# Two mixer stages in one program: a new order of transpositions, output product, weighted inputs and state in each supertile, and first loads issued beside the constants

## What is computed

```python
proj = norm(x) @ in_proj_w             # columns: z (1024) | x, B, C | dt
xBC  = silu(conv4(proj_xBC) + conv_b)  # causal, 4 taps, one filter per channel
dt   = softplus(dt + dt_bias); dA = exp(-exp(A_log) * dt)
state = state * dA_t + outer(dt_t * x_t, B_t)      # per head, along the sequence
y_t   = C_t @ state + D * x_t
out   = (rmsnorm(y) * silu(z)) @ out_proj_w        # A: rmsnorm(y * silu(z))
```

## Time and profile before

| what | value |
|---|---|
| median of 3 runs (lowest to highest) | 3190.09 us (3183.87 to 3195.75) |
| the profiled execution: its own time, its span | 3185.51 us, 3183.8 us |
| TensorE busy | 2839.6 us, 89% |
| VectorE, ScalarE, GpSimd busy | 65%, 39%, 31% |
| mean granted TensorE clock | 0.953 |
| mixer A: its first load, its last output product | 9.97 us, about 1210 us |
| mixer B: its first load, its last output product | 1461.90 us, about 2936 us |

### The profile page before, as it was taken

One profiled execution on the slowest core, in us unless ns is written; L12 is line 12 of the kernel. 1 busy time (PEld: TensorE's weight loads), 2 busy tenths in 40 slices (PEclk: granted clock), 3 DMA queues, 4 the chain that ended last, 5 costly groups with the idle time before them and its releaser, 6 DMA issues. The chain is left out here.

```text
span 3183.8 us, 54365 instructions
## 1 busy us (share of the span) xinstructions
PE 2839.6 (89%) x19824; PEld 1872.3 (59%) x19824; DVE 2071.5 (65%) x3697; ACT 1248.4 (39%) x2098; POOL 975.0 (31%) x618
## 2 busy tenths in 40 slices
PE   4999999999999996993899999999999999997896
PEld 4666666666666663453666666666666666664453
DVE  3565665665566562485777777877777777776267
ACT  2433434334443331331444444444444444443232
POOL 1232222332233230251233332333233333223135
PEclk9999999999999998996899999999999999998898
DMA  3000000000000005144000000000000000000533
GB/s 117 14 20 26 20 20 20 20 26 26 20 20 20 20 14 225 52 147 158 11 21 20 20 13 20 20 20 10 16 20 20 20 20 13 13 15 29 217 104 134
DMA packets 80673, 140.16 MB, mean 44 GB/s; under 512 B 18120, under 2 KB 18632, under 8 KB 79568
## 3 DMA queue, kind: packets, MB, share of 16 engines
q1 hardware_dynamic: 60048, 126.29, 11.2%
q10 hardware_dynamic: 20544, 12.79, 1.5%
HBM read 104.98 MB, written 33.55 MB: 44 GB/s over the span
## 5 line engine op out<-in xcount | busy, mean ns | idle before, releaser
L525 PE MATMUL work<-b_xnT,b_w_in 128*128 128x256 f32 x2304 | 564.6, 397 | 39.9 <-DVE b_state L1096 29.2
L525 PE MATMUL work<-a_xnT,a_w_in 128*128 128x256 f32 x2176 | 505.0, 388 | 10.0 <-DVE a_w_out L1227 5.8
L525 PEld LDWEIGHTS work<-b_xnT,b_w_in 128*128 128x128 f32 x2304 | 434.5, 195 | 127.8 <-DVE b_state L1096 36.0
L525 PEld LDWEIGHTS work<-a_xnT,a_w_in 128*128 128x128 f32 x2176 | 411.6, 193 | 83.1 <-issue 18.1
L1081 DVE TENSOR_TENSOR b_decay<-b_decay,b_gt 128x1024 f32<-128x1024 f32 x256 | 340.1, 1366 | 27.4 <-ACT b_decay L799 23.4
L799 ACT ACTIVATE b_decay<-seg 128x1024 f32<-128x1024 f32 x256 | 251.6, 1022 | 201.6 <-PE seg L649 200.9
L960 DVE SCALAR_TENSOR_TENSOR b_cv<-b_pre,b_conv_w,b_cv 128x256 f32<-128x256 f32 x480 | 249.6, 548 | 58.8 <-ACT b_cv L745 50.9
L1286 POOL TENSOR_TENSOR a_y<-a_y,a_skip 128x1024 f32<-128x1024 f32 x32 | 106.5, 3327 | 548.2 <-DVE a_y L1070 548.2
L1251 POOL TENSOR_TENSOR rhs<-b_l_side,of_head 128x1024 fp32r<-128x1024 f32 x32 | 83.2, 2600 | 609.3 <-DVE b_l_side L1050 609.3
L630 PE MATMUL work<-a_w_out,a_yz 128*128 128x512 f32 x512 | 248.8, 642 | 21.8 <-ACT a_xnT L729 18.1
L630 PE MATMUL work<-b_w_out,b_yz 128*128 128x512 f32 x512 | 230.8, 604 | 23.7 <-ACT b_xnT L729 15.6
(11 more groups left out here) (309 smaller groups left out, 4733.4 us busy)
## 6 DMA issues: line engine op xcount, KB each, us to landing
f_d_w<-in_L_ffn_d_w SPq DMA_DIRECT2D x4, 4096.0 KB, 24.0
f_x_in<-x_mid ACTq DMA_DIRECT2D x12, 1024.0 KB, 5.9
a_x_in<-in_L_attn_a_x SPq DMA_DIRECT2D x16, 512.0 KB, 3.7
a_x_res<-in_L_attn_a_x SPq DMA_DIRECT2D x32, 256.0 KB, 2.6
x_mid<-a_x_res SPq DMA_DIRECT2D x32, 256.0 KB, 2.0
f_x_res<-x_mid SPq DMA_DIRECT2D x8, 1024.0 KB, 5.5
f_bc_w<-x_mid SPq DMA_DIRECT2D x8, 1024.0 KB, 5.4
b_x_in<-x_mid SPq DMA_DIRECT2D x16, 512.0 KB, 3.6
```

The costliest lines, as they stand in the source:

```text
L525: mm = nc.tensor.matmul(dst, w_in[:, k, col:col + m], xnT[:, k, :], start=(k == 0), stop=(k == KD - 1))
```

## The change

1. TensorE's head becomes `xnT0, pout, xnT1, ident0, small1` (then `dt`). `pout` now has the bank of `prt`, `xnT1` that of `xnT0`, `small1` that of `pout`, and `dt` that of `xnT1`. `ident0` was after the first projections. ScalarE does `slot_exp(0,1)` between its two copies.
2. `state0` comes before the last `ydiag` steps of tile 0, and `state_add(0)` before `gate(0)`.
3. VectorE makes `xdt` of tile 0 right behind `masked_gt`, and that of tile 1 ahead of the first `slot_mult`.
4. `w_out` is multiplied by `norm_w` in the first supertile, at the place of `out_add`; TensorE waits for it before the first output product only.
5. A's `x_in` and `w_in` are issued on SyncE's queue inside the block of constants, and A's six vectors on ScalarE's queue there. The loads of `masks`, of F's 12 vectors and of B's six vectors go to SyncE's queue behind the second `x_in` and the first residual load of A. B issues no vector loads at its start. Both prologues transpose and copy `xn` before they wait for weights or vectors.

```diff
+def load_vectors(eng, dst, w, H, loaded):
+    for name in ("dt_bias", "A_log", "D"):
+        eng.dma_start(dst[name][:], w[name].rearrange("(a h) -> a h", a=1).to_broadcast([P, H])).then_inc(loaded, 16)
...
+def load_in(sp, x_in, w_in, xs_src, w, x_loaded, xbc_loaded):
+    sp.dma_start(x_in[:], xs_src[0]).then_inc(x_loaded, 16)
+    sp.dma_start(w_in[:, :, E:], w["in_proj"].rearrange("(t p) n -> p t n", p=P)[:, :, E:]).then_inc(xbc_loaded, 16)
...
     with nc.Block() as block:
+        @block.sync
+        def _(sp):
+            w = weights[mixers[0].tag]
+            load_in(sp, early["x_in"], early["w_in"], early["xs_src"], w, early["x_loaded"], early["xbc_loaded"])
+            load_z(sp, early["w_in"], w, early["z_loaded"])
...
+                load_vectors(act, c["vectors"][m.tag], weights[m.tag], m.H, c["vectors_loaded"][m.tag])
...
-                    + (["xnT0", "xnT1"] if nxt else []) + (["pout"] if prev else []) + ["small1"])
+                    + (["xnT0"] if nxt else []) + (["pout"] if prev else []) + (["xnT1"] if nxt else [])
+                    + ["ident0", "small1"])
...
-                if p == 0:
-                    steps += ["ident0"]
+                if p + 1 == NP:
+                    steps += state_steps(0)
                 steps += [f"ydiag0.{2 * p}", f"ydiag0.{2 * p + 1}"]
-            steps += (["z0a"] if nxt else []) + state_steps(0)
+            steps += ["z0a"] if nxt else []
...
                 load_x(1)
                 load_res(0, 0)
+                if later:
...
+                        load_ffn_vectors(sp, c["ffn"], c["ffn_w"], c["ffn_loaded"])
+                        load_vectors(sp, c["vectors"][later.tag], c["weights"][later.tag], later.H,
+                                     c["vectors_loaded"][later.tag])
...
+                        if isinstance(i, int) and i == 0:
+                            pe.wait_ge(w_out_ready, 1)
...
+                run(prologue(), pro_steps[:2])
                 pe.wait_ge(xbc_loaded, 16)
...
-                pe.wait_ge(w_out_ready, 1)
                 pe.wait_ge(c["masks_loaded"], 16 * 16)
...
                         xnT_copy(sec, 0)
+                    slot_exp(sec, 0, 1)
+                    if nxt:
                         xnT_copy(sec, 1)
-                    slot_exp(sec, 0, 1)
...
                     masked_gt(sec)
+                    make_xdt(sec, 0)
...
-                    make_xdt(sec, 0)
+                    make_xdt(sec, 1)
                     slot_mult(sec, 0, 0)
...
                     slot_mult(sec, 0, 1)
-                    make_xdt(sec, 1)
                     if prev:
                         out_add(sec, "pout", i - 1, 1)
+                    else:
+                        norm_into_w_out()
...
+                                state_add(sec, 0)
                                 gate(sec, 0)
```

More of the change, by code:

```diff
@@ L188, in build_constants, with mixer_phase @@
     return c
-def mixer_phase(nc, sig, before, cfg, c, first_mixer, psum, x_src, x_dst, w):
+def mixer_phase(nc, sig, before, cfg, c, early, later, psum, x_src, x_dst, w):
     H, HP, N, NS = cfg.H, cfg.HP, cfg.N, cfg.slots
@@ L213, in sb @@
             return ctx.enter_context(nc.sbuf_tensor(f"{cfg.tag}_{name}", shape, dt))
-        w_in = sb("w_in", [P, KD, cfg.proj])
+        w_in = early["w_in"] if early else sb("w_in", [P, KD, cfg.proj])
         w_out = sb("w_out", [P, KE, DM])
-        conv_w = sb("conv_w", [P, NB, TAPS])
-        conv_b = sb("conv_b", [P, NB])
-        norm_w = sb("norm_w", [P, KE])
-        dt_bias = sb("dt_bias", [P, H])
-        a_log = sb("a_log", [P, H])
+        conv_w, conv_b, norm_w, dt_bias, a_log, d_skip = (c["vectors"][cfg.tag][k] for k in (
+            "conv_w", "conv_b", "norm_w", "dt_bias", "A_log", "D"))
+        small_loaded = c["vectors_loaded"][cfg.tag]
         a_low, a_high = sb("a_low", [P, H]), sb("a_high", [P, H])
-        d_skip = sb("d_skip", [P, H])
-        x_in = sb("x_in", [P, 2, DM])
+        lhs, rhs = sb("lhs", [P, 2, P], F32R), [sb(f"rhs{k}", [P, 8, P], F32R) for k in range(2)]
+        x_in = early["x_in"] if early else sb("x_in", [P, 2, DM])
         x_res = sb("x_res", [P, 2, DM])
@@ L509, in _ @@
                 load_res(0, 0)
+                if later:
+                    for b in range(4):
+                        for q in range(4):
+                            sp.dma_start(c["masks"][32 * q:32 * q + 32, b], c["masked_bf"][32 * b:32 * b + 32]
+                                         ).then_inc(c["masks_loaded"], 16)
+                    with nc.allow_non_contiguous_dma(reason="small vectors"):
+                        load_ffn_vectors(sp, c["ffn"], c["ffn_w"], c["ffn_loaded"])
+                        load_vectors(sp, c["vectors"][later.tag], c["weights"][later.tag], later.H,
+                                     c["vectors_loaded"][later.tag])
                 before.clear(sp)
@@ L1128, in out_add, with norm_into_w_out @@
                                                    ).then_inc(out_done, 1)
+                def norm_into_w_out():
+                    dve.wait_ge(out_loaded, 16)
+                    for k in range(KE):
+                        ins = nc.vector.tensor_scalar(w_out[:, k, :], w_out[:, k, :], norm_w[:, k:k + 1], None, ALU.mult)
+                    ins.then_inc(w_out_ready, 1)
                 def supertile(sec, prev, nxt):
@@ L1224, in _ @@
                 exponent_sides(0)
-                dve.wait_ge(out_loaded, 16)
-                for k in range(KE):
-                    ins = nc.vector.tensor_scalar(w_out[:, k, :], w_out[:, k, :], norm_w[:, k:k + 1], None, ALU.mult)
-                ins.then_inc(w_out_ready, 1)
                 supertile(first(), False, True)
@@ L1894, in build, with first_mixer_buffers @@
         }
-        c = build_constants(nc, ctx, part("L0_ffn_"))
         mixer_signals, ffn_signals = Signals(nc, ctx, "m"), Signals(nc, ctx, "f")
         route = [x0] + x_mid[:len(STAGES) - 1] + [y]
+        weights = {"a": part("L0_attn_a_"), "b": part("L0_attn_b_")}
+        first = ExitStack()
+        def first_mixer_buffers():
+            return {"masked_bf": first.enter_context(nc.sbuf_tensor("masked_bf", [P, 4, P], BF16)),
+                    "x_in": first.enter_context(nc.sbuf_tensor("a_x_in", [P, 2, DM], F32)),
+                    "w_in": first.enter_context(nc.sbuf_tensor("a_w_in", [P, KD, mixer_a.proj], F32)),
+                    "xs_src": x0.rearrange("(s j p) d -> s p j d", p=P, j=2),
+                    "x_loaded": mixer_signals("x_loaded"), "xbc_loaded": mixer_signals("xbc_loaded"),
+                    "z_loaded": mixer_signals("z_loaded")}
+        c = build_constants(nc, ctx, part("L0_ffn_"), (mixer_a, mixer_b), weights, first_mixer_buffers)
         for k, stage in enumerate(STAGES):
@@ L1900, in build @@
             if stage == "A":
-                mixer_phase(nc, mixer_signals, ffn_signals, mixer_a, c, True, psum, src, dst, part("L0_attn_a_"))
+                with first:
+                    mixer_phase(nc, mixer_signals, ffn_signals, mixer_a, c, c["early"], mixer_b, psum, src, dst, weights["a"])
             elif stage == "B":
-                mixer_phase(nc, mixer_signals, ffn_signals, mixer_b, c, False, psum, src, dst, part("L0_attn_b_"))
+                mixer_phase(nc, mixer_signals, ffn_signals, mixer_b, c, None, None, psum, src, dst, weights["b"])
             else:
```

76 lines of the change are left out of this document (38 added, 38 removed).

## The result

The changed kernel takes 3009.26 us, the median of 4 runs (3007.08 to 3011.85). The kernel before took 3189.41 us beside it (4 runs, 3183.87 to 3195.75). The ratio is 0.9435, with a 95% interval from 0.9416 to 0.9454: 180 us less, where 152 had been forecast. The time lies a microsecond above the low end of the range. The profiled execution took 3011.85 us (span 3010.1), against 3185.51 before: 173.7 us less. The comparison by stages is made between these two.

A forecast was written before the change was run, and what follows sets the result against it. TensorE was taken to bound both loops. Waits 82, clock 30, prologue ends 12, start of B 15.5 and start of A 12 sum to 151.5 us off 3185.5: 3034, or 3038 as median; range 3008 to 3100.

The forecast's parts named there:

- start of B: B's first projection no longer waits for vectors landing at 1489.48, only for `w_in`: 15.5 us gained.
- waits in the loops: TensorE's waits for the `xnT` copy, `out_add` and `state_add` go in both loops: 82 us, ends 60 and 87.
- clock in the loops: Falls of TensorE's clock behind waits cost 39.9 us; a quarter stays: gain 30 us, ends 0 and 45.
- ends of the prologues: TensorE no longer waits for `w_out` there: 6 us in A, 8 in B, together 12 after the multiplications, ends 6 and 14.
- start of A: Loads issued inside the block of constants bring A's first projection to 25 to 29 us: gain 12, ends 8 and 18.
- Head, TensorE's side: At each supertile's head, `pout` hides the `xnT` copy, 33.7 us; the waits of `dt` for `out_add` go, 25.5 us.
- the cover of 0.3 us in A: In A's head VectorE finishes its last `slot_mult` 0.3 us before `pout` would end, so `out_add` is hidden.
- a late VectorE: Rival: VectorE is late for `out_add`, `small1` waits, 0.9 us in 28 supertiles, 25 us come back: 3063, chance 0.14.
- State of tile 0: `state0` and its add moved earlier give `z0b` its bank in time; B's waits for `state_add`, 27.3 us, go.
- a wait of `state0b` and a late `rs0` reader: New delays in B's loop behind ScalarE's copy and the convolutions: 0.3 us per supertile, 4 us in all.
- The second rival: The clock falls in each loop supertile's head, 1.7 us each; the 30 us gain becomes a loss of 8: 3076, chance 0.14.

## Why the prediction was right, and where its sizes were off

The sign, the mechanism and the range held, the range by a microsecond and with luck: the stages for which the forecast had no term lost 8.6 us, and without that loss the time would lie below its low end. The start of B left the bounds of its own term. The forecast's terms against the stages measured:

| term | forecast | measured |
|---|---|---|
| waits in the loops | 82 (60 to 87) | 86.6 |
| clock in the loops | 30 (0 to 45) | 39.9 |
| busy time at full clock | none | 11.2 |
| ends of the prologues, with the first supertiles | 12 (6 to 14) | 4.6 + 7.4 − 2.4 + 1.3 = 10.9 |
| start of B | 15.5 (13 to 18) | 19.1 |
| start of A | 12 (8 to 18) | 14.5 |
| the two F, last supertiles, end | none | −8.6 |
| sum | 151.5 | 173.6 |

**Head, TensorE's side.** Right: no wait for the copy, none for `out_add`, the cover of 0.3 us in A measured 0.35. In B the slot multiplication started later than reckoned, behind both halves of `xdt(1)` and the first slot, and the margin was 0.24 us instead of 1.0. It held in both. What the prediction made too little of is what stood on it: it priced a late VectorE at 25 us; the run with the old `xdt` order lost 118. The 0.9 us assumed for it there was 1.2 and 2.3, and the clock, which that rival left out, cost more than the wait.

**State of tile 0.** The 27.3 us went, and so did the falls behind them (13 us in the run with the step undone). The 4 us put down for a wait of `state0b` and a late `rs0` reader did not come: that is nearly the whole of 86.6 − 82.

**The clock.** This is the step that was mis-sized. A quarter of the falls was to stay: none stayed, 39.9 us against 30 (48, by the second profile of the kernel before). The reason given, the row in which `small1` and `dt` were followed by half clock, read the row for its products; it had half a microsecond of waiting in it, behind a longer wait at 590 us. The runs separate the two. The same head with one pause more falls in every supertile of A; with 32 transpositions more and no pause more, in none; with 0.4 us of pause among the small products and `ident0` gone from them, in 4 of 28. The second rival (a fall in each head, 3076 us), which the rule of the Trainium skill on transpose mode, cited above, would give, is refuted by the changed kernel and by the run with more transpositions.

**Busy time at full clock.** A term that was missing: TensorE's busy time of an undisturbed supertile fell by 0.48 and 0.32 us. The forecast took a wait's own length for its cost; 11.2 us on 86.6 come on top, and their cause stays open.

**Ends of the prologues.** At the transpositions the gain was 4.6 + 7.4 = 12.0 us, where 6 + 8 had been forecast. And the multiplications were said to cost 1.6 us in A and nothing in B where they went. They took 5.68 and 4.92 us, against 3.26 and 3.25 in the run that has them later: at the new place GpSimd works beside them, for 3.0 us in A (state and skip part) and for 1.9 in B (state), at the later one it doesn't. `small_sums(1)` behind them made TensorE wait 4.7 and 3.9 us. The run that moved them won back 4.8 us of TensorE's wait in A's first supertile and 5.6 us of the length of B's.

**Start of B.** 19.1 instead of 15.5: `w_in` landed 3.8 us sooner behind the first load. Less competition "may add 2", the forecast said; that it is the vectors' loads, now gone from beside it, is likely, but no run puts them back alone.

**Start of A.** The model was right: the block of constants ends for all together, and at 16 us (18 had been taken), since `norm_w` took 7.44 us to issue instead of 12.27. The run that takes `norm_w` out of the block shows it: its first projection starts at 17.00. The changed kernel's starts at 23.29, ahead of the 25 to 29 forecast.

**F.** Nothing of F's code was touched, and it gave back 7 us. The forecast had no term for a stage that enters with its falls at other points.

## What to carry to other kernels

Look at each wait of the bounding engine twice: for its length, and for what the clock does behind it. Here a wait of 1.2 to 2.3 us per supertile cost from half its length to more than its whole length again in falls (13 us on 26, 43 on 50, 63 on 51), any one of several was enough for that, and only taking out the last of them gave a loop without a fall. So the parts of such a change can't be judged one by one. And where a product is moved into a gap as a cover, the reader of its result on the other engine must have been freed first. Under the old head the reorder of VectorE leaves A's wait for `out_add` at 6.7 us and goes with a drop of B's from 18.8 to 5.7; under the new head, going without it costs 118 us.

## What the runs showed of the hardware that was not expected

- In these runs pauses brought TensorE's clock down, small work did not. A pause of 1.6 to 1.9 us ahead of the output product gave a fall in 22 of 28 supertiles; one of 1.2 us among small products in 11 of 14, one of 2.3 us there in 14 of 14; 7.2 us of transpositions and small products without a pause in none. Pauses that are alike do not all end alike: B's 14 of 1.6 us gave eight falls.
- A stage whose code is the same differs by where its falls come, and repeatably: the second F took 223.2 and 223.6 us in the two profiles of the kernel before and 227.1 to 228.2 in all others.
- Eight multiplications of 128x512 on VectorE took 3.26 us alone, 4.92 with 1.9 us of GpSimd's work beside them and 5.68 with 3.0: they lost 1.7 and 2.4 us, 0.8 to 0.9 of the time shared.
- A load of small elements can hold its queue in the issue itself: 7.44 us for the norm weights, behind five other loads on ScalarE's queue and beside `w_in`, but 0.58 us for the same load on SyncE's queue at 26.72 us. In the first case it held the end of the block for every engine.
